# First attention: row-maximum scores of two heads in two halves of the partitions, wider loads, denominators moved by DMA

## The chip, the cores and the metric

The kernel runs on one core of a Trainium2 chip. The metric is the device time of one execution in microseconds. A core has five engines that run side by side: TensorE (PE, its weight loads shown as PEld), VectorE (DVE), ScalarE (ACT), GpSimd (POOL) and SyncE (SP). Here SP issues the DMAs, which 16 DMA engines carry out.

## The reference, cut to what matters

Four blocks follow one another on x of 4 x 1024 x 128: an attention, a layer of experts, a second attention with a top-k mask, a second layer of experts. The change concerns the first, with 16 heads of 8 dimensions:

```python
q = x @ Wq + bq;  k = x @ Wk + bk;  v = x @ Wv + bv      # x after layernorm
q, k, v = (split_heads(q), split_heads(k), split_heads(v))
scores = jnp.einsum('bhqd,bhkd->bhqk', q, k) / jnp.sqrt(jnp.asarray(HEAD_DIM, dtype=x.dtype))
scores = jnp.where(causal, scores, WHERE_CONST)
probs = jax.nn.softmax(scores, axis=-1)
ctx = jnp.einsum('bhqk,bhkd->bhqd', probs, v)
out = ctx @ Wo + bo
```

## The kernel before, in words

`project` writes q and k to DRAM, each split into three bfloat16 terms of falling size (`q_parts`, `k_parts`), so that the nine products of terms add up to a float32 product. `attention0` then works in 16 rounds (`ITERS`); a round is one batch row and G = 4 heads. A head's eight dimensions times nine pairs of terms make `STACK` = 72 rows of `qs` and `ks`, in which the terms stand repeated. Three buffers of 4 x 1024 columns each (`half`) hold the heads of three rounds.

Each round has two kinds of scores. For the softmax the row maxima are needed first: TensorE computes blocks of up to 128 x 512 scores with the queries on the partitions (`S`, line 643, and line 646 for the causal corner), VectorE takes their maxima (line 773) into `mx`. `top` (line 766) joins them, TensorE transposes it (line 687), VectorE splits the negated maximum into three terms (`parts`, lines 781 to 793), and three DMAs (`store_max`, line 594) write these as rows 72 to 74 of `qs`, whose partners in `ks` are ones. Then the second kind: blocks with the keys on the partitions (`ST`, lines 656 and 659), which come out with the maximum already taken off. ACT takes the exp (line 706), and TensorE multiplies with v (line 673, `O`), four heads in four strips of 32 columns; v has a column of ones that gives the denominators. At the end of each half of the queries VectorE copies `O` to `num` (line 799), a matmul with `den_row` spreads the denominators over the partitions (lines 679 and 694, `extra`), VectorE takes reciprocals of 128 x 64 eight times (line 805), GpSimd multiplies (line 724), and SP moves the result to `packed` (line 616).

The order is written out by hand. A round is 48 slots (`NB_`). In slot p every engine does its share of block p: TensorE one maximum block and one `ST` block, plus `O` every fourth slot. The maximum blocks run 72 slots ahead (`AHEAD`): slots 0 to 23 hold the second half of the blocks of round it + 1 (list `A` from its middle), slots 24 to 47 the first half of round it + 2. `A` goes from the longest rows to the shortest. Before slot 24 TensorE waits for `kq_in`, the load of round it + 2. Before slot 0 it waits for `max_in`, the stored maxima. An `ST` block has two buffers, so TensorE may write block p when exp p - 2 is done. An `S` block has three.

SP's queue goes round by round in `step`: the load of q and k for round it + 2 (18 DMAs of 8 partitions, rows of 1024 columns; it waits for the scores of slot 0), v for round it + 1, the maxima of round it + 1, the packing of round it - 1. DMAs issued by SP wait behind each other on each DMA engine that they use. TensorE's rounds 1 to 13 are a hardware loop, and rounds 0, 14 and 15 are written out; SP's are all written out.

`setup` loads the weights; Wq and Wk of this attention go straight to their place.

## Time and profile before

| what | value |
|---|---|
| median of 3 runs | 4006.72 us (4006.63 to 4008.45) |
| the profiled execution | 4011.69 us, its span 4009.8 us |
| TensorE busy | 2731.8 us, 68% of the span |
| VectorE busy | 2881.5 us, 72% |
| ScalarE busy | 2582.6 us, 64% |
| GpSimd busy | 1755.7 us, 44% |
| exp of the first attention, line 706 | 768 of them, 359.7 us busy |
| row maxima, line 773 | 768 of them, 387.7 us busy |

The busy times are means over stages with different limits. The first attention takes some 740 of the 4009.8 us, and the change touches it and the setup alone; so its worth has to be read from windows of that stage. A TensorE matmul is pipelined and its end is modelled: the distance from one start to the next says more than its duration.

### The profile page before, as it was taken

To read this page: it belongs to the slowest core of one execution; us is meant where nothing else is said; L and a number is where in the kernel's file an instruction comes from. 1 tells how busy PE (TensorE), PEld (TensorE's weight loads), DVE (VectorE), ACT (ScalarE), POOL (GpSimd) and SP (SyncE) were. 2 spreads that over 40 slices of the span, in tenths; PEclk is the share of its full clock that TensorE was granted. 3 is DMA by queue.
4 is the path that set the end of the run, shared out by engine and by line. 5 is a ranking of instruction groups with operands and counts; after the bars stand their busy time and mean duration, and the time that the engine had idled before them with its cause. 6 is when DMAs were issued, how large, how long until landed. Compare 5 with 4: busy or idle time off the path is not lost. (4 is left out here: it accounts for less than half of the span.)

```text
span 4009.8 us, 93044 instructions
## 1 busy us (share of the span) xinstructions
PE 2731.8 (68%) x25318; PEld 1636.3 (41%) x25318; DVE 2881.5 (72%) x10864; ACT 2582.6 (64%) x4340; POOL 1755.7 (44%) x4286
## 2 busy tenths in 40 slices
PE   3588888848736566655565666666665666665999
PEld 2133333325524344433343444444443444453665
DVE  6677777630263888887887888888887888864444
ACT  2155555523311889977787988898998999862222
POOL 3000000020011777765575776777776777752000
PEclk9599999968966677777676777778877877776999
DMA  3323223100012100001100001000001000000000
GB/s 113 39 30 39 33 34 39 19 4 24 18 43 56 25 8 4 7 4 23 17 4 4 7 4 28 13 4 7 4 12 29 7 4 6 5 1 27 6 8 8
DMA packets 131770, 77.04 MB, mean 19 GB/s; under 512 B 73287, under 2 KB 116055, under 8 KB 131463
## 3 DMA queue, kind: packets, MB, share of 16 engines
q1 hardware_dynamic: 131463, 74.32, 10.3%
q14 instruction: 282, 2.31, 0.2%
q8 instruction: 25, 0.41, 0.0%
HBM read 52.15 MB, written 19.14 MB: 18 GB/s over the span
## 5 line engine op out<-in xcount | busy, mean ns | idle before, releaser
L1127 PE MATMUL a_ST<-a_qs,a_ks 75*128 (+1 forms) x4096 | 678.6, 255 | 687.6 <-ACT a_eT L1171 675.9
L1227 POOL TENSOR_TENSOR a_near<-a_side,a_z 128x1024 int32<-128x1024 int32 x512 | 968.3, 1891 | 47.9 <-POOL a_side L1223 10.3
L1127 PEld LDWEIGHTS a_ST<-a_qs,a_ks 75*128 75x128 bf16 x4096 | 478.7, 118 | 815.3 <-issue 801.7
L1345 DVE TENSOR_SCALAR_CACHE_REDUCE a_z<-a_S,a_thr 128x1024 f32<-128x1024 f32 x512 | 650.9, 1271 | 82.5 <-issue 62.6
L1149 ACT ACTIVATE a_signs<-a_z,a_tiny 128x1024 bf16<-128x1024 f32 x512 | 587.5, 1147 | 99.1 <-DVE a_z L1345 86.2
L1142 ACT ACTIVATE a_signs<-a_S,search 128x1024 bf16<-128x1024 f32 x512 | 568.3, 1110 | 48.7 <-PE a_S L1079 48.7
L706 ACT ACTIVATE a_eT<-a_ST 128x512 f32<-128x512 f32 (+3 forms) x768 | 359.7, 490 | 368.9 <-PE a_ST L659 257.4
L1171 ACT ACTIVATE a_eT<-a_ST 128x1024 f32<-128x1024 f32 x512 | 516.2, 1008 | 9.5 <-PE a_ST L1128 9.5
L773 DVE TENSOR_REDUCE a_mx<-a_S 128x1 f32<-128x512 f32 (+3 forms) x768 | 387.7, 535 | 163.9 <-PE a_S L643 116.6
L1079 PE MATMUL a_S<-a_ks,a_qs 72*128 72x512 bf16 x1024 | 396.8, 477 | 129.9 <-DVE a_z L1345 73.7
L1164 ACT ACTIVATE a_mask<-a_z,a_cut_steep 128x1024 bf16<-128x1024 f32 x256 | 292.0, 1141 | 159.2 <-issue 126.6
L1095 PE MATMUL a_O<-a_eT,a_v 128*9 128x128 f32 x8192 | 374.1, 325 | 1.4 <-ACT a_oT L1177 1.4
L1128 PE MATMUL a_ST<-a_minus_b,a_mask 128*128 128x128 bf16 x2048 | 363.9, 266 | 0.0
L643 PE MATMUL a_S<-a_ks,a_qs 72*128 (+4 forms) x768 | 270.3, 356 | 113.2 <-DMA a_ks<-k_parts 82.2
L1128 PE MATMUL a_ST<-ident_b,a_mask 128*128 128x128 bf16 x2048 | 317.0, 244 | 0.0
L1095 PEld LDWEIGHTS a_O<-a_eT,a_v 128*9 128x9 f32 x8192 | 212.3, 103 | 246.8 <-issue 216.4
L724 POOL TENSOR_TENSOR ctxT<-a_num,a_rden 128x512 f32 (+1 forms) x32 | 40.6, 1269 | 606.2 <-DVE a_rden L805 606.2
L656 PE MATMUL a_ST<-a_qs,a_ks 128*128 (+4 forms) x768 | 257.3, 338 | 19.0 <-ACT a_eT L706 13.2
L1128 PEld LDWEIGHTS a_ST<-a_minus_b,a_mask 128*128 128x128 bf16 x2048 | 247.9, 121 | 0.0
L1128 PEld LDWEIGHTS a_ST<-ident_b,a_mask 128*128 128x128 bf16 x2048 | 230.1, 112 | 5.9
L1804 ACT ACTIVATE f_gate<-f_G 128x512 f32<-128x512 f32 x112 | 66.8, 597 | 238.7 <-PE f_W L1778 190.4
L1383 DVE MAX8 a_cand<-a_near 128x8 f32<-128x256 f32 x512 | 213.6, 417 | 0.0
(331 smaller groups left out, 5841.8 us busy)
## 6 DMA issues: line engine op xcount, KB each, us to landing
a_ks<-k_parts SPq DMA_DIRECT2D x288, 64.0 KB
a_qs<-q_parts SPq DMA_DIRECT2D x144, 64.0 KB
a_qs<-q_parts SPq DMA_DIRECT2D x288, 32.0 KB
a_qs<-a_flip SPq DMA_DIRECT2D x512, 0.8 KB
q_parts<-p_qp SPq DMA_DIRECT2D x48, 128.0 KB, 1.7
k_parts<-p_kp SPq DMA_DIRECT2D x48, 128.0 KB, 1.8
f_w<-L_ffn_W SPq DMA_DIRECT2D x16, 256.0 KB, 2.5
v_ones<-p_vst SPq DMA_DIRECT2D x8, 288.0 KB, 2.4
```

Of the source, the lines that this page charges most:

```text
L706: act.activation(eT[:, gi % 4, p % G, 0:hi - lo], ST[p % 2][:, 0:hi - lo], ACT.Exp, scale=SCALE0).then_inc(e_done, 1)
L773: dve.tensor_reduce(mx[:, lo // CW, j * IB + i:j * IB + i + 1], S[r % 3][:, 0:hi - lo], AX, ALU.max).then_inc(max_s, 1)
L1079: mm = pe.matmul(S[h % 2][:, lo:lo + CW], qa, ks[0:STACK, h * SEQ + lo:h * SEQ + lo + CW], start=True, stop=True)
L1095: mm = pe.matmul(O[32 * j:32 * j + HD + 1, :], v[:, kb, head], eT[:, h0 % RING + j, kb * P:(kb + 1) * P], start=(kb == 0), stop=(kb == IB ...
L1127: pe.matmul(ST[:, block_of], ks[:, hl * SEQ + kb * P:hl * SEQ + (kb + 1) * P], qa, start=True, stop=False)
L1128: mm = pe.matmul(ST[:, block_of], mask[:, hl % MASKS, block_of], minus_b[:, :] if hl % 2 == 0 else k.ident_b[:, :], start=False, stop=True)
L1142: act.activation(signs[:, h % 2, :], S[h % 2][:, :], ACT.Sign, bias=first[:, bass.ds(n, 1)], accum_out=sgn[0][:, one]).then_inc(cnt1, 1)
L1149: act.activation(signs[:, 2, :], z[:, hl % RING, :], ACT.Sign, bias=tiny[:, :], accum_out=sgn[1][:, hl:hl + 1]).then_inc(cnt2, 1)
L1164: act.activation(mask[:, hl % MASKS, :], z[:, hl % RING, :], ACT.Relu, bias=cut_steep[:, hl:hl + 1], scale=-STEEP).then_inc(mask_a, 1)
L1171: act.activation(eT[:, hl % RING, :], ST[:, :], ACT.Exp, scale=SCALE1).then_inc(e_done, 1)
L1227: pool.tensor_tensor(near[:, hl % 2, :].bitcast(I32), side[:, one].bitcast(I32).broadcast_to([P, SEQ]), z[:, hl % RING, :].bitcast(I32), A ...
L1345: dve.tensor_scalar(z[:, h1 % RING, :], S[h1 % 2][:, :], thr1[:, one1], None, ALU.add, ALU.max, accum_out=zmax[:, one1]).then_inc(z_s, 1)
```

## The change

The scores for the maxima use rows 0 to 63 for one head of a pair and rows 64 to 127 for the other, with eight of the nine products of terms; the two matmuls of a pair go to different partitions of the array and to different `S` buffers, of which there are four now (`extra` gives up its place). The ninth product stands in the eight rows of the other half, so `ST`, which uses all 128 rows, has all nine. For heads to lie so that two neighbours are contiguous in DRAM, `setup` reorders the columns of Wq and Wk and the two biases, by VectorE copies and one more transpose. A load has 16 DMAs instead of 18, with rows of 2048 columns, 24, 16 or 8 partitions each. `A` goes from the shortest rows to the longest. The three maxima DMAs become six. Denominators: a DMA gathers the four rows of 512 into 128 x 16, VectorE takes one reciprocal of that, a DMA writes it to DRAM, and four DMAs read it back onto eight partitions each; the matmuls with `den_row` go. These DMAs stand in SP's queue between the others, each behind its wait. TensorE's loop and SP's steps are all written out, in constants.

```diff
@@ setup
-                 (k.wq[0][:, :], inp["L0_attn_Wq"]), (k.wk[0][:, :], inp["L0_attn_Wk"]),
+                 (raw_qk[:, 0, :], inp["L0_attn_Wq"]), (raw_qk[:, 1, :], inp["L0_attn_Wk"]),
-                 (k.bq[0][:, :], col(inp["L0_attn_bq"])), (k.bk[0][:, :], col(inp["L0_attn_bk"])),
+                 (raw_rows[0:1, :], row(inp["L0_attn_bq"])), (raw_rows[1:2, :], row(inp["L0_attn_bk"])),
...
+            pe.wait_ge(kept, 4)
+            pe.transpose(turned_g[:, E1 + E0 * FC0:], rows[:, :], k.ident[0:2, 0:2])
...
+            for x in range(4):
+                paired = lambda a: a[:, 32 * x:32 * x + 32].rearrange("p (a e d) -> p e d a", a=2, e=2)
+                in_order = lambda a: a[:, 32 * x:32 * x + 32].rearrange("p (e d a) -> p e d a", e=2, a=2)
+                dve.tensor_copy(in_order(rows), paired(raw_rows)).then_inc(kept, 1)
+                for s, w in enumerate((k.wq[0], k.wk[0])):
+                    dve.tensor_copy(in_order(w), paired(raw_qk[:, s, :]))
@@ attention0
-    A = [(i, j, lo, min(lo + CW, (i + 1) * P)) for i in range(IB - 1, -1, -1) for lo in range(0, (i + 1) * P, CW) for j in range(G)]
+    A = [(i, j, lo, min(lo + CW, (i + 1) * P)) for i in range(IB) for lo in range(0, (i + 1) * P, CW) for j in range(G)]
...
-        TOPAT, TURNAT = NA // 2, NA // 2 + 2
+        TOPAT, TURNAT = NA // 2, NA // 2 + 4
-        COPY0, DEN0, RDEN0 = G * FIRST_HALF + 4, G * FIRST_HALF + 18, G * FIRST_HALF + 20
-        COPY1, DEN1, RDEN1 = 4, 8, 10
-        RSTEPS = 8
+        COPY0, RDEN0 = G * FIRST_HALF + 4, G * FIRST_HALF + 22
+        COPY1, RDEN1 = 4, 23
+        DMAS_Q, DMAS_MAX, DMAS_REC = 16, 2 * SPLIT, G + 1
+        col = lambda j: (j % 2 * 2 + j // 2) * SEQ
...
             def load(x):
-                for u in range(SPLIT):
-                    for y in range(SPLIT):
-                        rows = slice((u * SPLIT + y) * HD, (u * SPLIT + y + 1) * HD)
-                        for dst, src, s in ((qs, k.q_parts, u), (ks, k.k_parts, y)):
-                            sp.dma_start(dst[rows, bass.ds(half(x), G * SEQ)].rearrange("d (g t) -> d g t", g=G),
-                                         src[s, bass.ds(x * G * HD, G * HD), :].rearrange("(g d) t -> d g t", d=HD)).then_inc(kq_in, 16)
+                at_x = slice(x * G * HD, (x + 1) * G * HD)
+                pair_of = lambda part, e: part.rearrange("(e d a) t -> e d (a t)", e=2, a=2)[e:e + 1]
+                pairs_of = lambda part, e: part.rearrange("y (e d a) t -> y e d (a t)", e=2, a=2)[:, e]
+                for e in range(2):
+                    cols = slice(half(x) + e * 2 * SEQ, half(x) + (e + 1) * 2 * SEQ)
+                    for u, n in ((0, 3), (1, 3), (2, 2)):
+                        at = 64 * e + u * SPLIT * HD
+                        sp.dma_start(qs[at:at + n * HD, cols], pair_of(k.q_parts[u, at_x, :], e).broadcast_to([n, HD, 2 * SEQ])).then_inc(kq_in, 16)
+                        sp.dma_start(ks[at:at + n * HD, cols], pairs_of(k.k_parts[0:n, at_x, :], e)).then_inc(kq_in, 16)
+                    at = 64 * (1 - e)
+                    sp.dma_start(qs[at:at + HD, cols], pair_of(k.q_parts[2, at_x, :], e)).then_inc(kq_in, 16)
+                    sp.dma_start(ks[at:at + HD, cols], pair_of(k.k_parts[2, at_x, :], e)).then_inc(kq_in, 16)
...
+            def gather(x, hf):
+                sp.wait_ge(oc, 2 * x + hf + 1)
+                sp.dma_start(den16[:, hf, :], num[HD::32, hf, :].rearrange("j (b c) -> j b c", c=16)).then_inc(den_in, 16)
+
+            def spread(x, hf):
+                sp.wait_ge(rec_s, 2 * x + hf + 1)
+                sp.wait_ge(ctx_s, 2 * x + hf + 1)
+                sp.dma_start(k.den_rows[hf].rearrange("j (b c) -> (j b) c", c=16), rec16[:, hf, :]).then_inc(rden_in, 16)
+                sp.wait_ge(rden_in, 16 * (DMAS_REC * (2 * x + hf) + 1))
+                for j in range(G):
+                    sp.dma_start(rden[32 * j:32 * j + HD, hf, :], k.den_rows[hf, j:j + 1, :].broadcast_to([HD, CW])).then_inc(rden_in, 16)
...
+            def step(it):
+                if it + 2 < ITERS:
+                    sp.wait_ge(score_s, NA * it + (AHEAD + 2))
+                    load(it + 2)
+                if it > 0:
+                    gather(it - 1, 1)
+                if it + 1 < ITERS:
+                    sp.wait_ge(vx_s, 2 * it + 1)
+                    load_v(it + 1)
+                if it > 0:
+                    spread(it - 1, 1)
+                gather(it, 0)
+                if it > 0:
+                    pack(it - 1)
+                if it + 1 < ITERS:
+                    store_max(it + 1)
+                spread(it, 0)
...
+                if x is not None and p % 2 == 0:
...
+                    for j in (j0, j0 + 1):
+                        rows = slice(64 * (j % 2), 64 * (j % 2) + 64)
+                        mm = pe.matmul(S[j][:, 0:hi - lo], qs[rows, half(x) + col(j) + i * P:half(x) + col(j) + (i + 1) * P],
+                                       ks[rows, half(x) + col(j) + lo:half(x) + col(j) + hi], start=True, stop=not diag)
...
-            dve.memset(qs[64:P, :], 0.0)
-            dve.memset(ks[64:P, :], 1.0)
+            for rows, odd in ((slice(64, P), 0), (slice(0, 64), 1)):
+                by_head = lambda a: a[rows, :].rearrange("d (x e t) -> d x e t", e=2, t=2 * SEQ)[:, :, odd, :]
+                dve.memset(by_head(qs), 0.0)
+                dve.memset(by_head(ks), 1.0)
...
-                        ins = dve.reciprocal(rden[:, hf, cols], extra[:, cols])
+                        dve.reciprocal(rec16[:, hf, :], den16[:, hf, :]).then_inc(rec_s, 1)
```

## Rows read from the trace of the kernel before

**Rows 1.** ACT's timeline: start, us, engine, line, operation, shapes [idle before <-its releaser].

```profile
177.44 0.60 ACT L706 ACTIVATE a_eT<-a_ST 128x512 f32<-128x512 f32 x1 [77.40 <-PE a_ST L659]
```

**Rows 2.** Windows: length, busy of PE, PEld, DVE, ACT, POOL, clock, DMA share, GB/s.

```profile
220.20:241.00 20.80, 16.98 (x135) 7.10 (x133) 14.72 (x36) 11.40 (x25) 1.56 (x2) 1.00 0.51 64
241.00:262.80 21.80, 20.30 (x130) 7.27 (x129) 17.47 (x37) 11.27 (x25) 1.50 (x2) 0.92 0.06 9
...
763.90:781.60 17.70, 15.91 (x132) 6.66 (x130) 14.51 (x35) 11.17 (x25) 1.58 (x3) 1.00 0.05 8
781.60:798.10 16.50, 13.88 (x93) 4.17 (x94) 4.49 (x12) 10.54 (x25) 1.50 (x2) 1.00 0.07 10
798.10:812.40 14.30, 12.16 (x89) 3.79 (x88) 4.82 (x10) 10.56 (x24) 1.56 (x2) 1.00 0.07 10
812.40:828.80 16.40, 13.49 (x93) 3.94 (x97) 3.44 (x8) 10.56 (x25) 1.27 (x1) 1.00 0.00 1
```

**Rows 3.** Windows, 300 to 700 us, the row maxima of line 773 alone.

```profile
300.00:700.00 400.00, 232.59 (x462) 0.97 0.29 36
```

**Rows 4.** Groups by line, 300 to 700 us: busy, mean ns | idle before.

```profile
L805 DVE RECIPROCAL a_rden<-a_extra 128x64 f32<-128x64 f32 x155 | 84.1, 543 | 0.0
```

**Rows 5.** Waits, 180 to 830 us: us in total, times, longest.

```profile
PE a_S L643 <- DMA a_ks<-k_parts: 30.9, 13, 3.7
```

**Rows 6.** Timeline around slot 24 of round 1.

```profile
236.25 1.06 PE L673 MATMUL a_O<-a_eT,a_vx 128*32 128x512 f32 x8
...
237.25 0.23 PE L643 MATMUL a_S<-a_ks,a_qs 72*128 x1
...
240.23 0.39 PE L643 MATMUL a_S<-a_ks,a_qs 72*128 x1 [2.48 <-DMA a_ks<-k_parts]
...
240.46 0.38 PE L656 MATMUL a_ST<-a_qs,a_ks 128*128 x1
```

**Rows 7.** Timeline of the first load; SPq rows are issues of DMAs.

```profile
118.25 0.32 SPq L584 DMA_DIRECT2D a_qs<-q_parts  x1
...
124.48 0.40 SPq L588 DMA_DIRECT2D a_vst<-v_rows  x1
...
139.04 2.60 PE L643 MATMUL a_S<-a_ks,a_qs 72*128 72x512 bf16 x5 [51.30 <-DMA a_ks<-k_parts]
```

**Rows 8.** DMA, 139 to 160 us; queue: packets, MB, share of 16 engines.

```profile
DMA packets 722, 1.20 MB, mean 57 GB/s; under 512 B 144, under 2 KB 144, under 8 KB 720
...
q1 hardware_dynamic: 720, 1.18, 45.1%
```

**Rows 9.** DMA, 918.95 to 919.15 us, expert weights loading.

```profile
q1 hardware_dynamic: 26, 0.05, 69.7%
```

**Rows 10.** DMA, 1440 to 1452 us, second attention; the last row is issues.

```profile
DMA packets 61, 0.01 MB, mean 1 GB/s; under 512 B 60, under 2 KB 60, under 8 KB 60
...
a_qs<-a_flip SPq DMA_DIRECT2D x4, 0.8 KB
```

**Rows 11.** DMA issues, 90 to 850: count, KB each, median us to landing.

```profile
a_qs<-a_parts SPq DMA_DIRECT2D x48, 8.0 KB, 1.9
...
q_parts<-p_qp SPq DMA_DIRECT2D x3, 128.0 KB, 1.7
```

**Rows 12.** DMA, 251 to 254 us, while packing runs.

```profile
DMA packets 64, 0.13 MB, mean 44 GB/s; under 512 B 32, under 2 KB 32, under 8 KB 64
...
q1 hardware_dynamic: 64, 0.13, 31.5%
```

**Rows 13.** Timeline of SP's issues, 238 to 262 us.

```profile
248.00 1.78 SPq L594 DMA_DIRECT2D a_qs<-a_parts  x3
249.82 2.78 SPq L616 DMA_DIRECT2D packed<-ctxT  x4
```

**Rows 14.** Timeline, the end of the last round.

```profile
829.20 0.69 DVE L799 COPY a_num<-a_O 128x512 f32<-128x512 f32 x1 [4.41 <-PE a_O L673]
...
834.63 1.26 POOL L724 TENSOR_TENSOR ctxT<-a_num,a_rden 128x512 f32<-128x512 f32 x1 [8.48 <-DVE a_rden L805]
```

More of the change, by code:

```diff
@@ L131, in setup @@
         raw = ctx.enter_context(nc.sbuf_tensor("raw_w", [P, 4, D], F32))
+        raw_qk = ctx.enter_context(nc.sbuf_tensor("raw_qk", [P, 2, D], F32))
+        raw_rows, rows = (ctx.enter_context(nc.sbuf_tensor(x, [2, D], F32)) for x in ("raw_rows", "rows"))
         raw_b1 = ctx.enter_context(nc.sbuf_tensor("raw_b1", [E0 * FC0, P], F32))
@@ L139, in setup @@
         col = lambda a: a.rearrange("(p o) -> p o", o=1)
+        row = lambda a: a.rearrange("(o n) -> o n", o=1)
         every = lambda a: a.rearrange("(o n) -> o n", o=1).broadcast_to([P, D])
@@ L181, in _ @@
                                base=0, pattern=[[-HD, H], [0, HD]], channel_multiplier=1).then_inc(made, 1)
[L183 to L185 removed]
+            pool.wait_ge(made, 5)
             pool.affine_select(out=k.head_of[:, :], in_=k.head_of[:, :], compare_op=ALU.is_ge, fill=0.0,
@@ L591, in store_max @@
             def store_max(x):
-                sp.wait_ge(part_s, 4 * x + 4)
+                sp.wait_ge(part_s, PARTS * x + PARTS)
                 for s in range(SPLIT):
-                    sp.dma_start(qs[STACK + s:STACK + s + 1, bass.ds(half(x), G * SEQ)].rearrange("o (c q) -> o c q", q=P),
-                                 parts[:, s, :]).then_inc(max_in, 16)
-            def step(it):
-                more = not (isinstance(it, int) and it + 2 >= ITERS)
-                if more:
-                    sp.wait_ge(score_s, NA * it + (AHEAD + 1))
-                    load(it + 2)
-                if not (isinstance(it, int) and it + 1 >= ITERS):
-                    sp.wait_ge(vx_s, 2 * it + 1)
-                    load_v(it + 1)
-                    store_max(it + 1)
-                if it > 0:
-                    pack(it - 1)
+                    for e in range(2):
+                        at = (HD if e else STACK) + s
+                        sp.dma_start(qs[at:at + 1, half(x) + e * 2 * SEQ:half(x) + (e + 1) * 2 * SEQ].rearrange("o (c q) -> o c q", q=P),
+                                     parts[16 * e:16 * e + 16, s, :]).then_inc(max_in, 16)
+            def gather(x, hf):
[8 more added lines that the diff above has]
+                    sp.dma_start(rden[32 * j:32 * j + HD, hf, :], k.den_rows[hf, j:j + 1, :].broadcast_to([HD, CW])).then_inc(rden_in, 16)
             def pack(x):
@@ L626, in _ @@
                 step(it)
+            gather(ITERS - 1, 1)
+            spread(ITERS - 1, 1)
             pack(ITERS - 1)
             sp.wait_ge(packed_s, 16 * G * ITERS)
-            sp.wait_ge(max_in, 16 * SPLIT * ITERS)
+            sp.wait_ge(max_in, 16 * DMAS_MAX * ITERS)
             sp.wait_ge(v_in, 16 * ITERS)
@@ L655, in slot @@
                     diag = lo == kb * P
-                    mm = pe.matmul(ST[p % 2][:, 0:hi - lo], ks[:, bass.ds(half(it) + j * SEQ + kb * P, P)],
-                                   qs[:, bass.ds(half(it) + j * SEQ + lo, hi - lo)], start=True, stop=not diag)
+                    mm = pe.matmul(ST[p % 2][:, 0:hi - lo], ks[:, half(it) + col(j) + kb * P:half(it) + col(j) + (kb + 1) * P],
+                                   qs[:, half(it) + col(j) + lo:half(it) + col(j) + hi], start=True, stop=not diag)
                     if diag:
@@ L675, in slot @@
                     mm.then_inc(pv, 1)
-                if p == DEN1 and live(before(it)):
-                    pe.wait_ge(oc, 2 * it)
-                    pe.wait_ge(rden_s, 2 * it - 1)
-                    pe.matmul(extra[:, :], k.den_row[:, :], num[:, 1, :], start=True, stop=True).then_inc(den_s, 1)
-                x = topped(it, p, TURNAT)
-                if x is not None:
-                    pe.wait_ge(top_s, x + 1)
-                    if not (isinstance(x, int) and x < 2):
-                        pe.wait_ge(rden_s, 2 * x - 2)
-                    elif x == 1:
-                        pe.wait_ge(part_s, 4 * x)
-                    pe.transpose(extra[0:G * IB, 0:P], top[:, :], k.ident[:, :]).then_inc(turn_s, 1)
-                if p == DEN0 and live(it):
-                    pe.wait_ge(oc, 2 * it + 1)
-                    if isinstance(it, int) and it + 1 >= ITERS:
-                        pe.wait_ge(rden_s, 2 * it)
-                    else:
-                        pe.wait_ge(part_s, 4 * it + 6)
-                    pe.matmul(extra[:, :], k.den_row[:, :], num[:, 0, :], start=True, stop=True).then_inc(den_s, 1)
-            run(slot, pe)
+            for it, ps in [(None, range(-AHEAD, 0))] + [(it, range(NB_)) for it in range(ITERS)] + [(ITERS, range(NB_ // 2))]:
+                for p in ps:
+                    slot(it, p)
         @block.scalar
```

99 lines of the change are left out of this document (52 added, 47 removed).

## The prediction

> **What bounds the kernel now.** I read the page first: its chain of work that ended last covers 7% of the span, so it says nothing of this change. All that the diff touches lies in the first attention and in the setup ahead of it. So I cut the first attention by its own pattern. One round is 48 slots (four heads of one batch row), and it falls into two halves: slots 0 to 23 and 24 to 47. The first exp of round 0 starts at 177.44 [rows 1] and that of round 14 at 763.9 [rows 2], so a round takes 586.5/14 = 41.9 us.
>
> The windows by half round [rows 2] show what fills it. Its first two rows are round 1: 20.8 and 21.8 us. The next two are round 14, which has no load to wait for and in its second half no row-maximum scores: 17.7 and 16.5 us. The last two are round 15, with no such scores at all: 14.3 and 16.4 us, though ACT computes only 10.6 us of each. That last pair is the floor of the transposed score, exp and context product alone: PE writes a score block, ACT takes the exp, PE may only then write the block after the next. No edit makes this part itself shorter, except for the denominator matmuls in it.
>
> What lies between floor and round is VectorE and a transfer. VectorE spends 232.59 us of 400 on the row maxima [rows 3] and 84.1 us on the reciprocals [rows 4]: at 41.9 us a round 24.4 and 8.8 us. With two copies of 0.69 [rows 14] and the splits it is busy 33 to 35 of 41.9 us, so it sets the pace wherever reciprocals lie between maxima. And at slot 24 TensorE waits for the next-but-one group's q and k: 30.9 us in 13 waits [rows 5]; in round 1 it stood 2.48 us there [rows 6]. The load is issued at slot 0 and is needed at slot 24, 20.8 us later. The first load, alone, took from 118.25 to 139.04, also 20.8 us [rows 7].
>
> **The change, part by part.**
>
> *Reciprocals.* Per round 16 pieces of 64 columns (8.8 us) go and two of 16 columns come, at most 0.54 each (the price of a 64-column one [rows 4]), likely 0.2. The two denominator matmuls of 512 columns go as well: each takes TensorE about as long as the 1.06 us of the context product beside them [rows 6]. VectorE is then busy 26 to 27 us a round and no longer sets the pace.
>
> *Scores in two halves.* Today a 512-column score takes 0.23 us of TensorE from its start to the next one's (240.23 to 240.46 [rows 6]). A first half gets 10,752 columns after the change (the order of blocks is reversed), a second half 7,680: 4.8 and 3.4 us one after another, 2.4 and 1.7 us if the two heads of a pair truly run side by side. No row shows two row halves at once. The nearest shows column strips: eight passes of up to 512 columns end within 1.06 us [rows 6], where eight times 0.23 would be 1.84. I take full overlap; the other bound is none. The causal matmuls stay, 12 and 20 of 128 columns, at 0.06 each 0.7 and 1.2 us.
>
> *Compute of a half after the change.* First half: floor 14.3, less 1.1 for the denominators, plus 2.4 and 0.7: 16.3 us. Second: 16.5 - 1.1 + 1.7 + 1.2 = 18.3 us. I do not take the scores as hidden, though ACT is the one that waits in the floor; that leaves up to 3 us on the fast side.
>
> *The loads.* This is the part that decides. Now a load is 18 DMAs, each 32 rows of 2 KB on 8 partitions. The window of the second load shows 720 packets, 144 of them small, that is 8 small ones a DMA, beside 576 rows [rows 8]. The small ones are the counts that each engine adds when done: 8 of the 16 DMA engines work. Their packets took 0.451 x 16 x 21 = 151.5 us, less the small ones some 0.25 us for 2 KB; an undisturbed 2 KB packet took 0.697 x 16 x 0.2 / 26 = 0.086 us [rows 9]. So eight engines writing the same eight partitions slow one another to a third.
> After the change a load is 16 DMAs of 4 KB rows. Twelve have a source whose outermost dimension is 3 or 2 (the broadcast copies of q, the terms of k) and four have 8. Does the outermost dimension decide how many engines work? The second attention has such a transfer: 3 destination rows, 12 source rows. Its four DMAs leave 60 packets: 48 pieces and 12 small ones, three each [rows 10]. So it does: 3 engines, not 12.
> The Trainium skill says the same (page "DMA: Bandwidth & Descriptors", section "Why a DMA increments its semaphore by 16 and not by 1"): a DMA uses the largest number up to 16 that divides the slowest dimension of both sides. With that rule the coming loads run on 3, 2 and 8 engines; without it, on the 8 of today or more. The trace agrees, 3 per DMA.
> The first engine thus carries per load: twice (8+8+8+8+8+8+1+1) = 100 rows of 4 KB. At two undisturbed 2 KB packets, 0.172 us a row: 17.2 us. With 1.9 us from issue to landing as for a small DMA [rows 11] a load takes 19.1 us. The bytes are as before, the engines fewer, each of them faster: 19.1 for 20.8 us. The upper bound of a row is the 4 KB packet of the packing DMAs, SBUF to SBUF: (0.315 x 16 x 3 - 0.3)/32 = 0.46 us [rows 12]. I take 0.172, since three engines write different partitions and the packing's eight write the same ones.
>
> *The round.* The load starts when slot 0's scores are done, some 0.4 us into the round. Its landing frees slot 24, and the gather of the denominators, queued behind it on the same engines, frees VectorE at slot 23. So the first half lasts 19.5 us (compute 16.3 is hidden below it), the second 18.3: 37.8 us. Is SP's chain shorter than the second half? Its issues cost 0.35 from DRAM (18 in 6.23 us [rows 7]), 0.60 from the split maxima, 0.70 for packing [rows 13]; a write lands after 1.7 us, a small load after 1.9 [rows 11]. From the landed gather: reciprocal 0.3, write 1.7, four loads 1.4, last landing 1.55, normalizing 1.3 [rows 14], packing 2.8, six stores of maxima 3.6 (they land at 14.0 us, needed at 18.3), second write 1.7, four loads 1.4: 15.8 us. It fits, with 2.5 us to spare. If it didn't, the next load would start late, and every us would cost 14.
> Saved: 41.9 - 37.8 = 4.1 us over 14 rounds, 57 us.
>
> *The rest.* Rounds 14 and 15: 17.7 to 16.3, 16.5 to 15.4, 14.3 to 13.2, 16.4 to 15.3: -4.7. Head: first load -1.7; 24 early maxima become 3,072 columns lighter, at the mean price of 0.5 us for 384 columns [rows 3] at most -4, I take -3. Tail: from the last copy to the last normalizing 5.4 us [rows 14] against 0.7 + 1.9 + 0.3 + 1.7 + 1.4 + 1.55 = 7.6: +2.2. Setup: twelve copies of 32 columns ahead of a transpose, two of one column behind it, two more memsets: +1 to +4, taken as +2. TensorE's loop is written out 16 times instead of looping; round 0, written out already, took about as long as the others (windows and boundaries above), so I give it nothing; its fetches are the risk.
> Sum: -57 - 4.7 - 1.7 - 3 + 2.2 + 2 = -62 us. The profiled execution took 4011.69 us, 1.9 beyond its span of 4009.8; the median is 4006.72, 5 us less, which changes none of the differences. 4006.7 - 62 = 3945 us.
>
> **The rivals.**
> *The compute halves are better than I took them.* The scores fit in TensorE's waits for ACT; second half 16 us, round 35.9 (SP's chain of 15.8 just fits). -84 - 5 = 3917 us. For it: in the floor ACT is idle a third of the time. Against: round 14's first half, with scores, was 3.4 us longer than round 15's, though VectorE explains most of that.
> *The loads use more engines.* With 8 or 12 engines a load takes about 10 us and vanishes: round 16.3 + 18.3 = 34.6, 3900 us. Against it: the three counts per DMA [rows 10].
> *TensorE doesn't gain.* The halves don't overlap, and each change between a 64-row and a full matmul costs something: 24 pairs of changes a round. The first half hides it below the load, the second grows by 1.7 + 12 x 0.1 = 2.9 us: round 40.7, 3985 us. For it the Trainium skill (page "TensorEngine Tiling (Array Packing)", section "Tiling Modes"): changing the tiling mode drains TensorE. A product in strips of 1.06 us was followed after 0.99 us by a full one (236.25 to 237.25 [rows 6]), so a drain there, if any, is under 0.1 us.
> *Slower: three engines are too few.* One mechanism: at 100 rows in a row on one engine, the load sets the round. It breaks even when a load takes 23.6 us, that is at 0.217 us a row. At the 0.25 us that a 2 KB packet takes today it would be 26.9 + 0.4 + 18.3 = 45.6 us a round, 4054 us; at the 0.46 of the packing [rows 12], 66.6 us, 4350. For it: today's packets take three times their undisturbed time. Against: that is eight engines in one place, and in the change it is three in three.
> *Nothing moves:* rows near 0.217 us.
>
> **How the numbers follow.** Forecast 0.43; compute better 0.18; more engines 0.09; TensorE without gain 0.12; too few engines 0.13; nothing 0.05. Below 0.2% (8 us, about what a measurement can tell here) nothing can be said. Faster: 0.43 + 0.18 + 0.09 + 0.12 = 0.82, same 0.05, slower 0.13. The range from 3890 to 4010 holds all but the slow case and the edges; the likeliest case alone spans 3925 to 3965.
>
> **What the profile after would show.** Per load 352 packets, 64 of them small, against 720 and 144. A load from the first issue to the first score of slot 24 at 19 us, DMA share near 0.2 instead of 0.5 at about 65 GB/s. A round of 37.8 us: TensorE waiting some 3 us for q or k at slot 24, VectorE waiting beside it for the gather. Reciprocals of 16 columns, 32 in all. The prediction is wrong if a 4 KB packet takes over 0.2 us, if SP reaches the next load late, or if the second half of a round stays near 21 us with no transfer to wait for.

## The result

| what | before | after |
|---|---|---|
| median | 4007.59 us (4 runs, 4006.63 to 4010.39) | 3968.73 us (4 runs, 3967.3 to 3969.99) |
| span of the profiled execution | 4009.8 us | 3968.2 us |

The ratio is 0.9902, 95% interval 0.9885 to 0.9919: 38.9 us faster, where 62 were forecast. The forecast of 3945 us is 24 us too low; its range of 3890 to 4010 holds the result.

**Where the time went.** Windows of the whole stages, first the kernel before, then after: length, busy PE, PEld, DVE, ACT, POOL, clock, DMA share, GB/s.

```profile
98.80:840.70 741.90, 609.97 (x4176) 231.43 (x4176) 531.20 (x1139) 360.91 (x769) 50.09 (x66) 0.91 0.26 32
...
1287.60:3595.00 2307.40, 1440.56 (x18048) 948.35 (x18048) 1942.03 (x8666) 1985.41 (x3201) 1582.64 (x4101) 0.74 0.06 10
```

```profile
98.90:811.70 712.80, 558.99 (x4064) 182.16 (x4112) 435.49 (x917) 355.44 (x769) 50.85 (x67) 0.88 0.14 38
...
1260.40:3554.40 2294.00, 1448.46 (x18048) 955.91 (x18048) 1955.03 (x8666) 1980.29 (x3201) 1583.55 (x4101) 0.74 0.06 11
```

The first row of each fence is the first attention, the second row the second attention. The first attention gave 29.1 us. The second attention, in which no line was changed, gave 13.4; the rest of the span moved by 1 us in all. So of the 41.6 us between the two spans only 29 answer to the forecast's 62.

**The round.** The first exp starts at 176.32, that of round 14 at 737.4: 561.1/14 = 40.1 us a round, against 41.9 before and 37.8 forecast. Windows by half round after, which answer to [rows 2]: rounds 1, 4, 14 and 15.

```profile
215.60:236.40 20.80, 15.87 (x125) 5.44 (x124) 14.88 (x30) 11.11 (x25) 0.29 (x1) 0.96 0.21 64
236.40:255.70 19.30, 18.80 (x132) 5.93 (x133) 11.28 (x28) 11.09 (x24) 2.77 (x3) 0.87 0.11 18
334.80:356.50 21.70, 15.83 (x125) 5.44 (x124) 14.87 (x30) 11.09 (x24) 0.29 (x1) 0.94 0.20 62
356.50:375.70 19.20, 18.59 (x132) 5.90 (x133) 11.30 (x29) 11.15 (x25) 2.77 (x3) 0.89 0.10 17
737.40:753.30 15.90, 14.97 (x120) 5.01 (x119) 14.25 (x28) 11.01 (x25) 0.29 (x1) 1.00 0.06 11
753.30:768.80 15.50, 12.77 (x89) 3.80 (x92) 1.36 (x6) 10.56 (x26) 1.27 (x1) 1.00 0.11 18
768.80:782.80 14.00, 11.26 (x86) 3.36 (x85) 1.54 (x3) 10.52 (x24) 1.74 (x3) 1.00 0.03 7
782.80:798.00 15.20, 12.21 (x86) 3.47 (x87) 0.25 (x1) 10.45 (x25) 2.54 (x2) 1.00 0.11 18
```

The reader sees two things. Where no load stands in the way (round 14) a first half takes 15.9 us; with a load it takes 20.8 to 21.7. And the granted clock is below 1 in both halves of a round with a load, and 1.00 where there is none. The waits after, 180 to 830 us, which answer to [rows 5], name the load, and beside it the gather of the denominators, which is queued behind the load (us in total, times, longest):

```profile
DVE a_rec L844 <- DMA a_den<-a_num: 67.2, 16, 5.1
PE a_S L695 <- DMA a_ks<-k_parts: 64.9, 14, 5.3
```

30.9 us of TensorE's waiting for q and k have become 64.9. The load of round 4, SP's issues of it (start, length):

```profile
334.35 0.84 SPq L601 DMA_DIRECT2D a_qs<-q_parts  x1
335.23 0.78 SPq L602 DMA_DIRECT2D a_ks<-k_parts  x1
...
344.65 0.29 SPq L605 DMA_DIRECT2D a_ks<-k_parts  x1
344.99 0.63 SPq L622 DMA_DIRECT2D a_den<-a_num  x1
```

And its end on TensorE, timeline of the same kernel:

```profile
355.36 0.29 PE L695 MATMUL a_S<-a_ks,a_qs 64*128 64x128 bf16 x2 [5.27 <-DMA a_ks<-k_parts]
...
357.73 1.94 PE L728 MATMUL a_O<-a_eT,a_vx 128*32 128x512 f32 x8
```

From 334.35 to 355.36 are 21.0 us, where 19.1 were forecast. After 5.27 us of standing still the context product takes 1.94 us instead of the 1.06 of [rows 6]. Windows of the same stretch show why; the granted clock is the third number from the end:

```profile
350.00:355.40 5.40, 0.13 (x3) 0.04 (x2) 0.46 (x1) 0.60 (x1) 0.00 (x0) 0.88 0.12 43
355.40:357.40 2.00, 2.00 (x11) 0.75 (x11) 0.97 (x5) 0.88 (x2) 0.00 (x0) 0.50 0.06 6
357.40:359.40 2.00, 2.00 (x9) 0.20 (x8) 0.40 (x2) 0.80 (x2) 0.00 (x0) 0.50 0.14 33
359.40:361.40 2.00, 1.67 (x11) 0.55 (x8) 0.39 (x2) 0.60 (x2) 1.26 (x1) 0.62 0.04 4
361.40:375.70 14.30, 14.02 (x112) 4.80 (x112) 10.40 (x26) 8.86 (x21) 1.50 (x2) 1.00 0.11 17
```

TensorE comes back at 0.50, the lower of its two levels (1.2 GHz), and is at 2.4 GHz again some 5 us later.

### The profile page after: what moved, and what is told of

It reads as the page before. It is cut to its first block and busy times, and to the rows that moved or that the text cites. A ratio compares the mean times of both kernels' runs of the same rounds, so it can differ in the third digit from the quotient of the medians.

```text
span 3968.2 us, 90596 instructions
## 1 busy us (share of the span) xinstructions
PE 2687.0 (68%) x25207; PEld 1592.6 (40%) x25255; DVE 2800.6 (71%) x10656; ACT 2572.0 (65%) x4340; POOL 1756.9 (44%) x4285
## 5 line engine op out<-in xcount | busy, mean ns | idle before, releaser
L711 PE MATMUL a_ST<-a_qs,a_ks 128*128 128x512 bf16 (+3 forms) x720 | 240.3, 347 | 17.4 <-ACT a_eT L744 15.3
L695 PE MATMUL a_S<-a_ks,a_qs 64*128 64x512 bf16 (+3 forms) x768 | 137.7, 355 | 126.3 <-DMA a_ks<-k_parts 116.3
```

## The experiments

Ratios are to the kernel before, run in the same series (4008.28, 4014.32 and 4011.54 us in the three series). These medians lie up to 7 us apart, so a total set against the changed kernel's 3968.73 us, which is of another series, is no better than that; the profiles decide. Lengths of rounds are taken between the starts of first exps in the profile, over the first 14 rounds; where no load stands in the way, over rounds 1 to 13, because round 0 is longer.

**Without the loads**

```diff
-                    load(it + 2)
+                    if it + 2 < 3:
+                        load(it + 2)
```

with TensorE's wait cut to the three loads.

> The changed kernel, with the loads of q and k only for rounds 0 to 2; the rounds after them score what already lies in the three buffers (left out: the q and k of rounds 3 to 15, so the output is not the reference's). Everything else is issued as before. My theory: the first half of a round is set by the load, because TensorE stands 5.3 us in each of 14 rounds for it. Then 13 loads less are 13 x 5.3 = 69 us, and some more if the slow clock that follows each wait goes too: 3895 us (3880 to 3905) against 3968.7, and a round of about 34.5 us. Rival one: the wait moves to the denominators, which VectorE waits for as long as TensorE waits for the load (65.2 us in the chain of its waits): then less than 3 us a round goes, 3930 or more. Rival two: SyncE's chain of issues sets the round even without the load: first half above 18 us, 3925 or more.

Round 4 of it, both halves:

```profile
314.20:330.20 16.00, 15.32 (x124) 5.25 (x123) 14.31 (x29) 11.11 (x24) 1.54 (x3) 1.00 0.06 10
330.20:347.80 17.60, 17.25 (x132) 5.84 (x134) 12.67 (x30) 11.16 (x25) 2.35 (x2) 1.00 0.11 19
```

A round is 33.5 us (347.8 - 314.2 = 33.6), 6.6 less than in the changed kernel: in the mean of rounds 1 to 13 the first half is 5.1 us shorter (16.0 for 21.1), and the second 1.5 (17.5 for 19.0), at clock 1.00. Both rivals fall: neither the denominators nor SyncE's chain take over. (The 10.6 us of issues go with the load here; the version with the 8 rows outermost, below, has them and the same round.) The expected total failed for a reason outside the stage: 4164.59 us, ratio 1.0394 (1.0374 to 1.0413). The first attention is 87 us shorter, but other q and k change the data, and the second attention then runs its repair pass for tied thresholds more often (VectorE has 8968 instructions there instead of 8666) and takes 2573.9 us.

**More engines through stacked arrays**

```diff
-                        sp.dma_start(qs[at:at + n * HD, cols], pair_of(k.q_parts[u, at_x, :], e).broadcast_to([n, HD, 2 * SEQ])).then_inc(kq_in, 16)
+                        sp.dma_start(qs[at:at + n * HD, cols], rows_of(k.q_stack, q0, n)).then_inc(kq_in, 16)
```

`q_stack` and `k_stack` are written by `project`, with the terms of a pair of heads as 48 and 80 rows behind one another.

> The changed kernel, with the terms of q and k of the first attention stored by the projection in two stacked arrays (three copies of slots for q, five for k), so that every load of 24, 16 or 8 rows reads as many equal rows as it writes, and its 4 KB packets go over 12, 16 or 8 DMA engines instead of 2, 3 or 8. It needs nine stores a chunk in the projection instead of seven. Theory: the load is set by its packets on three engines (100 rows of 4 KB on the first, 0.16 us each, with gaps between the DMAs). Spread over more, it ends with its issues, 10.6 us, plus 1.9 for the last to land, 12.5 us, which lies below the 15.9 us of computing: 14 x 5.3 = 74 us less, some given back in the projection: 3900 us (3885 to 3925). Rival: the load is set by the issue of its 16 DMAs and their rows on SyncE, whichever engines carry them: then the wait stays above 3 us a round and the time at 3940 or more. Second rival: spread packets come with more descriptors and the issue itself grows, slower than 3968.7.

3866.69 us, ratio 0.9651 (0.9634 to 0.9667). TensorE no longer waits for q and k; the round is 33.5 us, as without loads. Two more things are in the total: `project` ends at 116.4 instead of 98.9 us, because of its stores, and the second attention takes 2273.7 us, some 20 less than in the changed kernel. VectorE runs one repair pass less there (two, where the changed kernel has three), for which the other order of summing is the only cause that I can name; it is not shown. The projection's price was underrated in the expectation, the repair pass not foreseen.

**Both heads of a pair in the same half**

```diff
+        head = (0, 2, 1, 3)
...
-                        rows = slice(64 * (j % 2), 64 * (j % 2) + 64)
+                        hd = head[j]
+                        rows = slice(64 * (hd % 2), 64 * (hd % 2) + 64)
```

and `col(hd)` for `col(j)` in what is read and where the maxima go.

> The changed kernel, with the order of the heads in a pair changed: heads 0 and 2, then 1 and 3, so that both row-maximum score matmuls of a pair read the same 64 partitions and can't run at the same time. Loads, waits and counts stay. Theory of the prediction: two heads in different halves overlap on TensorE, the two 512-column matmuls of a pair end within 0.39 us; without it TensorE has 1.7 us more in each half of a round. The first halves are hidden below the load, the second ones are not: 14 x 1.7 = 24 us, 3992 us (3980 to 4010). Rival: TensorE has room in the second half, set by ScalarE's exps or by VectorE, and the overlap is worth nothing there: 3969 (within 8 us).

3986.27 us, ratio 0.9947 (0.9932 to 0.9961): 18 us more than the changed kernel, between the two theories. The profiles show 9 us of it in the stage (721.9 for 712.8); a round is 40.4 us, against 39.6 to 40.1 in three kernels that do the same work there (the changed one and the two with no-ops and the kept tile, below). While the load sets the first half, only the second can show the overlap. It is 19.7 us in the mean of rounds 1 to 13, against 18.8 to 19.0 in those three, and that is near their spread.

**The old kernel with the new denominators alone** (old loads, old scores; gather, one reciprocal of 16 columns, spread, and SyncE's new order)

> The kernel before, with only the denominators changed: taken out of the copied sums by a DMA, inverted as 16 columns, stored and spread by DMAs, in SyncE's new order; its row-maximum scores and its loads stay. Theory: the first half of a round stays at the 20.8 us of the old load, and the second loses what VectorE saves (8 pieces of 0.54 us each and a 512-column float matmul on TensorE): 1.5 to 2 us a round, about 25 us, 3982 us (3970 to 3995) against 4007.6. Rival one: VectorE was hidden in the second half too: 4007 (within 8 us), and all of the 39 us come from the load and the scores. Rival two: the denominators give all of it: 3970 or less, and the new scores and loads are worth nothing.

4009.42 us, ratio 0.9996 (0.9985 to 1.0008): nothing, as rival one has it. But the profile shows that this zero is a sum. The round is 40.9 us, 1.0 less, and the stage 725.5 instead of 741.9; the second attention is 2324.5 instead of 2307.4 and takes it back, for a reason that stays open (see the no-ops below). The load hides the rest of the denominators' worth: TensorE waits 56.1 us for q and k, 30.9 before [rows 5].

**36 DMAs of 8 rows** instead of 16 of 24, 16 and 8 (each on 8 partitions, source and all else as it was)

> The changed kernel, with each load of q and k split into 36 DMAs of 8 rows of 4 KB instead of 16 DMAs of 24, 16 and 8 rows; same bytes, same packets, no change in the projection. My theory, after the version with stacked arrays: what made the load 21 us is that the DMAs of 24 and 16 rows run on three and two engines, which also holds up their issue (0.64 to 0.84 us each against 0.29 to 0.43 for those of 8 rows). On 8 engines 288 packets of 0.16 us are 5.8 us; the issue of 36 at 0.3 to 0.35 us is 11 to 12.6 us and sets the load: 13 to 14.5 us, below the 16 us that the first half computes. Round 33.5 us as in the version without loads, 14 x 6.6 = 92 us less than 3968.7: 3877 us (3868 to 3890). Rival: 36 issues and the rest of SyncE's chain (15.8 us in the changed kernel) don't fit the round: SyncE is the bound, a round above 35 us, 3895 or more. Second rival: small DMAs on 8 engines wait for each other as in the kernel before: the wait for the load stays above 3 us a round, 3925 or more.

3947.61 us, ratio 0.9833 (0.9819 to 0.9847), 21 us better than the changed kernel, where 92 were expected. Its issues (timeline of SP), and TensorE's wait for them:

```profile
362.56 0.28 SPq L602 DMA_DIRECT2D a_qs<-q_parts  x1
362.88 0.30 SPq L603 DMA_DIRECT2D a_ks<-k_parts  x1
...
367.58 1.77 SPq L602 DMA_DIRECT2D a_qs<-q_parts  x1
...
376.19 0.29 SPq L603 DMA_DIRECT2D a_ks<-k_parts  x1
```

```profile
381.44 0.23 PE L693 MATMUL a_S<-a_ks,a_qs 64*128 64x128 bf16 x2 [3.13 <-DMA a_ks<-k_parts]
```

13.9 us of issues, one every 0.34 us with one stall of 1.77, and 5 us more until TensorE is let go: 18.9 us. The issues are not all of it: they alone and the 1.9 us of a small load's landing [rows 11] would be 15.8. The 288 packets of 4 KB of this load take 0.371 us each in the mean of the trace (0.42 over 13 loads), twice the 0.187 of the changed kernel, and the last ends at 379.70, 3.2 us after the last issue. The wait stayed at 3.4 us a round (47.6 in 14), as the second rival had it; that the small DMAs wait for one another fits the slow packets. The round is 38.6 us (714.0 - 173.6 over 14).

**The same, both heads in the same half**

> The version with 36 DMAs of 8 rows, and in it the heads of a pair from the same half of the partitions (0 and 2, 1 and 3), so that no two row-maximum score matmuls overlap. With the load hidden, both halves of a round are set by computing. Theory: without the overlap TensorE has 0.21 us more for each pair of 512 columns and less for the narrower ones, 1.7 us in each half: a round of 33.5 + 3.4 us, 14 x 3.4 = 48 us more than the version with 36 DMAs, about 3925 us (3905 to 3940). Rival: TensorE is not the bound of the halves (ScalarE or VectorE is): within 10 us of the version with 36 DMAs.

3953.75 us, ratio 0.9850 (0.9835 to 0.9865), 6 us more. The load was not hidden, so this could not tell what the overlap is worth; the next pair can.

**The 8 rows outermost.** Sixteen DMAs as in the changed kernel, the source walked in another order:

```diff
-                pair_of = lambda part, e: part.rearrange("(e d a) t -> e d (a t)", e=2, a=2)[e:e + 1]
-                pairs_of = lambda part, e: part.rearrange("y (e d a) t -> y e d (a t)", e=2, a=2)[:, e]
+                pair_of = lambda part, e: part.rearrange("(e d o a) t -> e d o (a t)", e=2, a=2, o=1)[e]
+                pairs_of = lambda part, e: part.rearrange("y (e d a) t -> e d y (a t)", e=2, a=2)[e]
...
-  pair_of(k.q_parts[u, at_x, :], e).broadcast_to([n, HD, 2 * SEQ])
+  pair_of(k.q_parts[u, at_x, :], e).broadcast_to([HD, n, 2 * SEQ])
```

> The changed kernel with its 16 DMAs a load and its arrays as they are, but with the source of each DMA walked with the 8 rows of a head outermost and the copies or terms inside (8 x 3 and 8 x 2 instead of 3 x 8 and 2 x 8); the rows of a block stand in that order in the partitions, for q and k alike. Nothing else differs. Theory: which engines carry a DMA goes by its outermost count, so the DMAs of 24 and 16 rows now run on 8 engines as those of 8 rows do; SyncE isn't held up (0.35 us an issue instead of 0.64 to 0.84), the load takes 6 us of issues and ends in 10 to 13 us, below the 16 us that the first half computes. Round 33.5 us, no cost in the projection: 14 x 6.6 = 92 us less than 3968.7, 3877 us (3855 to 3890; 19 us lower if the other order of summing happens to spare the second attention one of its repair passes, as with the stacked arrays). Rival: the engines go by something else, the load stays at 21 us and the total within 8 us of 3968.7. Second rival: the 4 KB packets now come out of order with their neighbours, 0.33 us each as in the stacked version, 36 on each of 8 engines: 12 us, still hidden; if they take 0.5 us or more, the wait is back.

3870.81 us, ratio 0.9644 (0.9631 to 0.9657), 98 us better than the changed kernel by the two medians: this version beats both. Some 91 us are 14 rounds of 6.5, and 6.5 come before them: the first exp starts at 169.79 for 176.32. Round 4, and two issues of its load:

```profile
304.50:320.50 16.00, 15.47 (x126) 5.26 (x124) 14.33 (x29) 11.10 (x24) 0.95 (x3) 1.00 0.29 83
320.50:338.00 17.50, 17.49 (x134) 5.83 (x134) 12.49 (x30) 11.12 (x24) 2.46 (x2) 1.00 0.11 19
```

```profile
304.06 0.76 SPq L601 DMA_DIRECT2D a_qs<-q_parts  x1
...
314.13 0.30 SPq L605 DMA_DIRECT2D a_ks<-k_parts  x1
```

The page's count of packets, first of the changed kernel, then of this one:

```profile
DMA packets 137272, 80.07 MB, mean 20 GB/s; under 512 B 82345, under 2 KB 125115, under 8 KB 136939
```

```profile
DMA packets 138297, 80.08 MB, mean 21 GB/s; under 512 B 83370, under 2 KB 126140, under 8 KB 137964
```

1025 small packets more, with all else the same. With an outermost count of 3, 3 and 2, a load leaves 8 x 3 + 4 x 2 + 4 x 8 = 64 counts; with 8 throughout, 128; the difference over 16 loads is 1024. So the 24- and 16-row DMAs went from three and two engines to eight. The Trainium skill's rule on the slowest dimension (page "DMA: Bandwidth & Descriptors", section "Why a DMA increments its semaphore by 16 and not by 1") says the same, and the trace agrees. The expectation's other half failed: an issue still costs 0.67 to 0.76 us, so that cost does not come from engines that are behind. It goes with how the source is walked: the same 24 rows cost 0.30 to 0.43 us from the plain rows of the stacked arrays. 10.4 us of issues, and the last 4 KB packet ends at 316.27, 12.2 us after the first issue. The packets take 0.202 us in the mean, on eight engines as with the 36 DMAs, where they took 0.371. What differs is which rows the eight engines write at one time; that this is the cause is not shown. In the second half TensorE is busy 17.49 of 17.50 us, as far as the modelled ends of its matmuls can be trusted; the next run tests whether it is the bound.

**The 8 rows outermost, both heads in the same half**

> The kernel with the 8 rows outermost, and in it the heads of a pair from the same half of the partitions, so that no two row-maximum score matmuls overlap; the load is hidden in both. Theory: the overlap is worth 1.7 us in each half when nothing waits for the load: a round of 36.9 instead of 33.5 us, 48 us more than the kernel with the 8 rows outermost (35 to 60). Rival: the halves are set by ScalarE or VectorE, and the overlap is worth less than 10 us in all.

3910.59 us, ratio 0.9745 (0.9732 to 0.9759), 40 us more. Its round 4:

```profile
317.10:334.30 17.20, 17.14 (x126) 5.45 (x124) 14.26 (x29) 11.14 (x25) 0.29 (x1) 1.00 0.28 78
334.30:352.90 18.60, 18.59 (x134) 6.04 (x133) 12.43 (x31) 11.07 (x24) 2.78 (x3) 1.00 0.11 18
```

35.8 us a round, 2.3 more, 1.1 in each half where 1.7 were expected; TensorE is busy through both halves. Only the overlap on TensorE was taken away, and both halves are longer by it, so TensorE is the bound. It is not free of ScalarE: in the second half of the version with the overlap its weight loads wait 6.3 us for exps, under matmuls that still run. Groups by line, 300 to 700 us, the 512-column scores of the version with the overlap and of this one:

```profile
L695 PE MATMUL a_S<-a_ks,a_qs 64*128 64x512 bf16 x258 | 50.3, 386 | 0.0
```

```profile
L697 PE MATMUL a_S<-a_ks,a_qs 64*128 64x512 bf16 x264 | 79.5, 381 | 0.0
```

One alone takes as long in both (386 and 381 ns), but 258 of them, 99.6 us one after another, fill only 50.3 us with the overlap: two run fully side by side. Without it they are pipelined and fill 79.5.

**The old kernel without the loads, and the same with the new denominators** (both leave out the q and k of rounds 3 to 15)

> The kernel before, with the loads of q and k only for rounds 0 to 2 (left out: the q and k of rounds 3 to 15; the total is not to be compared, because other scores change what the second attention has to do; the length of a round is read from the profile). In the changed kernel without loads a round takes 33.5 us. Theory: the old computing round, with 128 rows a score matmul, sixteen reciprocal pieces of 0.54 us and two float matmuls for the denominators, is longer: 37 to 38.5 us, so that the change gives 4 us a round or more where no load stands in the way, and before 3.5 to 5 us of its 41.9 were the load's. Rival: the old computing round is 40 us or more: the load cost the kernel before next to nothing. Other rival: it is 34 to 35 us: the new scores and denominators were worth next to nothing.

> The kernel before with only the new denominators, and with the loads of q and k only for rounds 0 to 2 (left out: the q and k of rounds 3 to 15; the total is not to be compared, the length of a round is read from the profile). Without loads a round takes 38.6 us in the kernel before and 33.5 us in the changed one. This one says which part of the 5.1 us is whose. Theory: TensorE sets the halves, and the denominators take it two float matmuls of 512 columns a round, VectorE 16 pieces of 0.54 us that stand in its way once a half: 36.5 us (35.5 to 37.5), 2 us from the denominators and 3 us from the scores. Rival: 38.2 or more, the denominators are worth nothing even without the load. Other rival: 34 or less, they are worth all of it.

Each ran once. Their totals (4255.03 and 4204.7 us) hold other data, as said; the halves of round 4, first without, then with the new denominators:

```profile
334.90:353.00 18.10, 16.44 (x133) 6.97 (x132) 14.67 (x36) 11.29 (x25) 1.56 (x2) 1.00 0.05 7
353.00:373.50 20.50, 18.70 (x128) 7.26 (x130) 17.49 (x37) 11.26 (x26) 1.50 (x2) 1.00 0.05 8
```

```profile
320.40:336.80 16.40, 15.43 (x132) 6.66 (x130) 11.57 (x29) 11.05 (x25) 0.29 (x1) 1.00 0.06 8
336.80:355.00 18.20, 17.75 (x128) 6.87 (x128) 15.00 (x30) 11.25 (x25) 2.79 (x3) 1.00 0.10 17
```

| us a round | with its load | load left out or hidden |
|---|---|---|
| before | 41.9 | 38.6 |
| and new denominators | 40.9 | 34.6 |
| the whole change, loads on 3, 2 and 8 engines | 40.1 | 33.5 |
| the whole change, loads on 8 engines | 33.5 | |
| that, without the overlap | 35.8 | |

The denominators are worth 4.0 of the 5.1 us (2 were expected), and the rest of the change 1.1: the scores in pairs, their order, the fourth buffer, the program written out. The overlap alone is worth 2.3, and without it the changed kernel is 1.2 us slower than the old scores with the new denominators (35.8 for 34.6); which part of the rest costs that is not shown.

Nor do these runs say which engine the 4.0 us come from. With the new denominators TensorE is busy 33.2 us of a round instead of 35.1 and VectorE 26.6 instead of 32.2; both change at once.

**No-ops, and the tile kept,** both aimed at the second attention, which no edit touches and whose length yet differs: 24 no-ops on TensorE and on VectorE at the end of the first; and the 128 x 128 tile that the change removed allocated again, unused.

> The changed kernel, with 24 no-ops more on TensorE and 24 on VectorE at the end of the first attention; nothing else differs. In the profiles the second attention, which the change does not touch, took 2307.4 us before and 2294.0 after, 2297.1 with the pairs in the same half and 2324.5 in the kernel with the new denominators alone, a difference that grows evenly from head to head. Theory one: the pace of that stage hangs on where its instructions lie behind those of the first attention: then its length changes here by 5 us or more, either way, and the total with it. Theory two: it hangs on something else (the clock, the run, the arithmetic): the stage stays within 4 us of 2294.0, and the total within 6 us of 3968.7 (the no-ops themselves cost about 1 us).

> The changed kernel, with the 128 x 128 tile that the change removed allocated again but never used, so that every tile behind it lies where it lay before. Theory one: the even difference in pace of the second attention (2307.4 us before, 2294 to 2297 in all kernels made from the changed one) comes from where its tiles lie: then it takes 2305 us or more here and the total is 3976 us or more. Theory two: not from that: 2294 to 2300 us, the total within 6 us of 3968.7.

3965.07 us, ratio 0.9878 (0.9861 to 0.9895), and 3968.27 us, ratio 0.9893 (0.9878 to 0.9908). The second attention of each, then of the version with the 8 rows outermost:

```profile
1252.60:3550.00 2297.40, 1446.34 (x18048) 953.94 (x18048) 1955.47 (x8666) 1980.16 (x3201) 1583.57 (x4101) 0.74 0.06 10
```

```profile
1253.40:3547.20 2293.80, 1426.40 (x18048) 938.86 (x18048) 1955.55 (x8666) 1981.88 (x3201) 1589.47 (x4101) 0.75 0.06 11
```

```profile
1162.20:3456.20 2294.00, 1447.71 (x18048) 954.03 (x18048) 1955.51 (x8666) 1980.35 (x3201) 1583.54 (x4101) 0.74 0.06 11
```

Neither moved it. With the same number of repair passes, every kernel made from the changed one has 2294 to 2297 us there, the one before 2307, the one with the new denominators alone 2324. The tile's place is not the cause, nor do 24 no-ops matter. One thing in the traces goes with it. Ahead of one VectorE instruction, 512 times in the stage, the engine stands idle with nothing in the profile to wait for, for 119.8 us before and 100.3 after (the last number of each line; 116.5 to 122.9 in the four kernels with the old scores, 96.0 to 100.3 in every version of the changed kernel):

```profile
L1381 DVE MATCH_VALUE_LOAD a_rest<-a_best,a_cand 128x8 f32 x512 | 44.8, 87 | 119.8 <-issue 119.8
```

```profile
L1418 DVE MATCH_VALUE_LOAD a_rest<-a_best,a_cand 128x8 f32 x512 | 45.0, 88 | 100.3 <-issue 100.3
```

Why it stands there longer stays open.

## Why the prediction came out as it did

The mechanism was right: the denominators and scores take computing out of both halves, and the load on three engines becomes what ends the first half. So was the sign. The forecast of 62 us against 38.9 was off by the terms below, and part of its nearness is luck (the last point).

- **"A load takes 19.1 us" is the term that failed first.** It measured 21.0. The windows of the DMA queue show no packet before 335.9 and only small ones from 354.8: 1.6 us ahead, 0.6 behind, and 18.9 for the 100 rows of the first engine, 0.19 us each instead of 0.172. It is the packets that are slower: the 288 of 4 KB in this load take 0.187 us each in the mean of the trace, and 100 of them in a row are 18.7 us. They are unequal: half take 0.159 or less, and the mean is 0.219 from 336 to 340 us, 0.175 to 346, 0.214 to 350. Only the last stretch, where two engines have rows left, keeps to the assumed price in its mean. The DMA view from 350 to 354 us has 49 of 4 KB beside 18 small ones:

```profile
DMA packets 67, 0.20 MB, mean 50 GB/s; under 512 B 18, under 2 KB 18, under 8 KB 67
...
q1 hardware_dynamic: 67, 0.20, 12.7%
```

  0.127 x 16 x 4 / 49 = 0.166 us, with the small ones in it; 12.7% of 16 engines is two, without a pause. Why packets take longer earlier in the load stays open. In the first half this made 21.1 us in the mean of rounds 1 to 13, where 19.5 stood: 1.6 x 14 = 22 us.
- **The second half, 18.3 forecast, is 19.0 in the mean.** Its computing is even below the sum (17.5 without a wait), but the 5 us of standing still bring the lower clock with them, which the working left out: 0.7 x 14 = 10 us against the forecast, 1.5 x 14 = 21 against what was to be had. So a load that comes late cost more than its lateness, 6.6 us a round instead of 5.
- **Computing of a first half, 16.3, measured 15.9 to 16.0.** The two together, 34.6 against 33.5, were good to 3%; the rival's 16 us for a second half were not reached. (That rival's round adds 0.4 us twice: 19.5 + 16 is 35.5 and not 35.9, and its time 3912 us.) One part was mis-sized: each denominator matmul was taken at the 1.06 us of the context product, and the kernel before has them at 0.62 and 0.65 us in its groups by line, 300 to 700 us:

```profile
L679 PE MATMUL a_extra<-a_num,den_row 128*128 128x512 f32 x20 | 10.8, 620 | 0.0
L694 PE MATMUL a_extra<-a_num,den_row 128*128 128x512 f32 x18 | 10.1, 645 | 0.0
```

- **"Two heads truly run side by side", taken full, is shown:** 99.6 us of matmuls in 50.3. But the 2.4 + 1.7 us of that are worth 2.3 a round when TensorE is the bound, and less under the load. The rival of a TensorE that gains nothing is out: its second half of 21.2 us measured 19.0, and 17.5 at full clock.
- **VectorE "sets the pace wherever reciprocals lie between maxima"** is not shown. Without loads the denominators are worth 4.0 us a round, but TensorE lost work with them as well, and in that old round it is busy 35.1 us against VectorE's 32.2. The reciprocal of 16 columns took 0.25 us (0.2 taken).
- **Loads on 3, 2 and 8 engines** is shown by the packets. The rival of more engines had the prize about right, and the change did not reach it: with 8 engines the kernel takes 3871 us, where 3900 stood.
- **The rival of three engines too few** broke even at 23.6 us a load. At 21.0 the case lay nearer to it than the forecast had it.
- **SP's chain** fits as worked out: the next load is issued at 375.25, when the round's start allows it, and over the stage SP stands 39.6 us in 14 waits for that start. Its issue price was wrong, though: 10.6 us for 16 DMAs where 0.35 each were taken, hidden because the engines were slower still. In the version with 36 DMAs the issues are 13.9 of the load's 18.9 us.
- **The rest.** Rounds 14 and 15: -4.3 (-4.7 forecast; 60.6 against 64.9 us). Tail, from the last copy to the last normalizing, 798.68 to 805.74, 7.1 against 5.4 us: +1.6 (+2.2). Head: -1.3 (-4.7 with the maxima). Setup: +0.1 (+2), by the starts of the stage. Rounds 0 to 13: -25.3 (-57).
- **What no term had:** the second attention's 13.4 us. Without them the forecast would have missed by 37 and not by 24 us, so that much of its nearness is luck. Their cause is open.

## What to carry to other kernels

Before widening a transfer's rows, look at the outermost count of both sides: the engines that carry it go by that, and walking the same bytes in another order was worth two and a half times the change itself. What an edit is worth has to be read with the other limits away: the denominators gave 1.0 us a round under the load and 4.0 without it. And where TensorE stands still for a few us, count the slow clock behind it as well.

## What the runs showed of the hardware that was not expected

- After 5.3 us of standing still TensorE runs at 0.50 of its clock for 4 us and more (355.4 to 359.4), then at 1.00. In the version with the 8 rows outermost, where it never waits for a load, it has 1.00 in both halves of round 4.
- Issuing a DMA costs 0.3 to 0.46 us for 8 rows of 4 KB and 0.64 to 0.84 for 16 or 24 with a repeated source or several terms, whichever engines carry it; from the plain rows of the stacked arrays mostly 0.30 to 0.43 for as many rows.
- A 4 KB packet of a load takes, in the mean over 13 loads, 0.187 us in the changed kernel, 0.201 on eight engines with 16 DMAs, 0.36 from the stacked arrays and 0.42 on eight engines with 36 DMAs. From the first issue to the end of the last packet a load took 19.8, 11.8, 10.9 and 17.6 us: what more engines gave, slower packets could take back.
- An untouched stage of 2300 us ran 13 us faster behind one program and 17 slower behind another, spread over its whole length. A total within 0.5% is not proof of what the edited stage does; its own windows are.
- With one repair pass less (two for three) the second attention took 2273.7 us for 2294.0: 20 us that go with the pass, in a kernel whose edit was elsewhere.
